# Attention and GRU kernel: a group's projections spread over its four steps, other work moved with them

## The reference

```python
x = x + attn(cond_layer(x, 1, rms_weight, cond, Wk, Wo, ln_gamma, ln_beta), W_attn, b_attn, W_proj, b_proj)
x = x + ffn(gru(cond, x, W_ih, W_hh, b_ih, b_hh), weight, scale_weight, bias)
```

## Time and profile before

| | us |
|---|---|
| median of three runs (lowest, highest) | 452.37 (450.24, 454.48) |
| profiled execution | 452.29 |
| its span, first to last instruction | 450.5 |
| TensorE busy (share of the span) | 408.1 (91%) |
| VectorE busy | 327.2 (73%) |
| ScalarE busy | 220.1 (49%) |
| GpSimd busy | 141.4 (31%) |

### The profile page before, as it was taken

The page is one execution under the profiler, slowest core; times in us unless marked ns, Lnnn a source line. Parts: engine busy times, 40 slices in busy tenths (PEclk is TensorE's granted clock), DMA queues, the critical chain, the costliest instruction groups (busy, mean ns, idle before and its releaser), DMA issues.

```text
span 450.5 us, 14909 instructions
## 1 busy us (share of the span) xinstructions
PE 408.1 (91%) x6216; PEld 339.5 (75%) x6216; DVE 327.2 (73%) x971; ACT 220.1 (49%) x545; POOL 141.4 (31%) x202
## 2 busy tenths in 40 slices
PE   8899898988969799889798779899999999999994
PEld 6556676766847677768567569799999999999984
DVE  2586989698876966868867955658676677667665
ACT  6265546555455465645565453444444444444341
POOL 6763174664364534624566730000000000000000
PEclk9999999999999989899999999999999999999999
DMA  8942413123132041231212000001010101000001
GB/s 289 397 167 95 130 45 113 50 73 84 38 98 93 28 119 50 73 102 43 74 52 73 26 3 0 1 2 47 2 47 1 47 8 43 23 25 25 24 25 70
DMA packets 33251, 30.46 MB, mean 68 GB/s; under 512 B 3104, under 2 KB 28320, under 8 KB 33184
## 3 DMA queue, kind: packets, MB, share of 16 engines
q1 hardware_dynamic: 33184, 29.51, 19.8%
HBM read 16.92 MB, written 8.39 MB: 56 GB/s over the span
## 4 chain that ended last, share of the span: by engine, by line
PE 72%; DVE 15%; issue 5%; ACT 5%; POOL 1%; DVEq 0%; POOLq 0%
PE ps_s L1428 7%; PE ps_t L1428 6%; PE ps_o L1428 6%; PE ps_s L1327 6%; PE ps_m L1365 5%; PE ps_t L1260 5%; PE ps_s L1483 5%; PE ps_t L1483 4%; PE ps_a L1483 4%; PE ps_a L1260 4%; PE ps_m L1483 4%; PE ps_o L1345 4%; DVE pT L964 4%; DVE mx L956 2%; PE ps_m L1357 2%
## 5 line engine op out<-in xcount | busy, mean ns | idle before, releaser
L533 POOL TENSOR_TENSOR sc<-masked,mx 128x512 f32<-128x512 f32 x64 | 66.4, 1059 | 102.4 <-DVE mx L956 102.4
L1365 PE MATMUL ps_m<-oT,w_p 128*128 128x128 f32 x256 | 38.0, 293 | 11.4 <-ACT oT L572 11.4
L1365 PEld LDWEIGHTS ps_m<-oT,w_p 128*128 128x128 f32 x256 | 31.8, 195 | 18.3 <-ACT oT L572 18.3
L948 DVE COPY_PREDICATED masked<-kst,ps_s 128x512 f32<-128x512 int32 x64 | 43.7, 731 | 1.5 <-PE ps_s L1327 1.5
L639 ACT ACTIVATE sc<-sc 128x512 f32<-128x512 f32 x64 | 39.9, 624 | 8.8 <-POOL sc L533 8.5
L964 DVE STREAM_TRANSPOSE pT<-sc 128x512 f32<-128x512 f32 x64 | 41.4, 682 | 1.4 <-ACT sc L639 1.4
L1327 PE MATMUL ps_s<-kbd,qn 32*32 32x128 f32 x2048 | 38.4, 272 | 2.6 <-issue 2.4
L956 DVE TENSOR_REDUCE mx<-masked 128x16 f32<-128x512 f32 x64 | 39.7, 660 | 0.0
L747 ACT ACTIVATE zg<-ps_t,brz 128x128 f32<-128x128 f32 x64 | 20.1, 365 | 39.6 <-PE ps_t L1428 37.3
L1094 DVE SCALAR_TENSOR_TENSOR rg<-ps_o,vec,rg 128x128 f32<-128x128 f32 x64 | 19.5, 345 | 24.8 <-PE ps_o L1428 23.9
L1428 PEld LDWEIGHTS ps_s<-hT,w_hh 128*128 128x128 f32 x256 | 33.1, 191 | 4.9 <-DVE hT L1112 2.8
(11 more groups left out here) (161 smaller groups left out, 811.4 us busy)
## 6 DMA issues: line engine op xcount, KB each, us to landing
xf<-in_x_feat SPq DMA_DIRECT2D x8, 512.0 KB, 9.5
xg<-in_x_tok SPq DMA_DIRECT2D x8, 512.0 KB
kbd<-kn SPq DMA_DIRECT2D x64, 64.0 KB, 1.9
v_dram<-vn SPq DMA_DIRECT2D x16, 256.0 KB, 2.6
vbd<-v_dram SPq DMA_DIRECT2D x64, 64.0 KB, 2.0
out_feat<-ost SPq DMA_DIRECT2D x16, 256.0 KB, 2.0
w_qkv<-in_wqkv SPq DMA_DIRECT2D x1, 768.0 KB, 9.8
w_ih<-in_wih SPq DMA_DIRECT2D x1, 768.0 KB, 13.3
```

Source lines behind the costliest of these rows:

```text
L533: nc.gpsimd.tensor_tensor(shifted, kept, m.unsqueeze(2).to_broadcast([P, NH // 2, S]), ALU.subtract).then_inc(sc_sub, 1)
L948: nc.vector.copy_predicated(kept, keep.unsqueeze(1).to_broadcast([P, NH // 2, S]), ps_s[:, h * 512:(h + 1) * 512].rearrange("p (h k) -> p ...
L1365: last = nc.tensor.matmul(ps_m[:, E + m * P:E + (m + 1) * P], w_p[:, c, m * P:(m + 1) * P], oT[:, c, :], start=(c == 0), stop=(c == C - 1))
```

## The change

On TensorE, `work_ahead` becomes `keys`, `queries` and `values`, and their halves are spread over the four steps: keys 0 at i = 0; keys 1 and queries 0 at i = 1; queries 1 and values 0 at i = 2; values 1 at i = 3. The second half of each stands ahead of the output projection of its step. The block projection of group g+2 moves from i = 1 to i = 0 for g = 1 to 5, ahead of the output projection, and into a bank of `ps_t` instead of `ps_a`; the VectorE and ScalarE operations around it move with it. On VectorE the token statistics are cut in two: tiles 0 and 1 stay at the end of step 2, tiles 2 and 3 with the aggregation go to step 3, where the transposition of the probabilities comes ahead of the mask. The adds giving y now follow the transposition of step 2. `inverse_std` moves to i = 3. On ScalarE the second exp of step 0 goes ahead of `oT`. SP's queue is as before.

```diff
         proj_ps = ps_a[0:MH, 0:E]
         proj_ps_1 = ps_s[0:MH, 0:E]
+        proj_ps_ahead = ps_t[0:MH, 0:E]
...
+                    if i == 3 and g + 2 < NG:
+                        inverse_std(g + 2)
                     if n + 1 < NT:
                         softmax_shift(n + 1)
-                    if i == 2 and g + 2 < NG:
-                        inverse_std(g + 2)
                     if n - 1 in BY_POOL:
                         residual(n - 1, (n - 1) // GT, (n - 1) % GT)
...
                 if i == 0 and not last_group:
                     round_y(g + 1, 0)
                     round_y(g + 1, 1)
+                    softmax_exp(n, n % 2, 1)
                 if n > 0:
                     attn_out(n - 1)
-                softmax_exp(n, n % 2, 1)
+                if i > 0 or last_group:
+                    softmax_exp(n, n % 2, 1)
+                if i == 0 and 0 < g < NG - 2:
+                    round_proj(g + 2, proj_ps_ahead)
+                if i == 1 and not last_group:
+                    k_chunk(g + 1, 1)
+                if i == 2 and not last_group:
+                    q_chunk(g + 1, 1)
+                if i == 3 and not last_group:
+                    v_half(g + 1, 1)
                 if n - 1 in BY_POOL:
                     projection_out(n - 1)
-                if i == 0 and not last_group:
-                    k_chunk(g + 1, 0)
                 if i == 0 and g in (0, 2):
                     cond_exp(2 + g // 2)
                 if i == 0 and not last_group:
-                    k_chunk(g + 1, 1)
+                    k_chunk(g + 1, 0)
                 if i == 1 and not last_group:
                     q_chunk(g + 1, 0)
-                    q_chunk(g + 1, 1)
-                if i == 1 and g + 2 < NG:
+                if i == 1 and g == 0:
                     round_proj(g + 2, proj_ps)
                 if i == 2 and not last_group:
                     v_half(g + 1, 0)
-                    v_half(g + 1, 1)
...
                 norm_ahead = g + 2 < NG
                 if n > 0:
                     normalise(n - 1)
+                if i == 0 and 0 < g < NG - 2:
+                    select_blocks(g + 2)
...
                 if i == 0 and g + 1 < NG:
                     rest_of_y(g + 1)
+                if norm_ahead and i == 3:
+                    some_token_stats(g + 2, 1).then_inc(bn_done, 1)
+                    mean_and_variance(g + 2)
+                    transpose_probs(n, n % 2)
                 if n + 1 < NT:
                     softmax_mask(n + 1, (n + 1) % 2)
-                if norm_ahead and i == 2:
-                    add_proj(g + 2, ps_a)
...
-                transpose_probs(n, n % 2)
+                if i == 0 and 0 < g < NG - 2:
+                    rest_of_proj(g + 2, proj_ps_ahead)
                 if i == 1 and g in (0, 2):
                     keep_weights(2 + g // 2)
-                if norm_ahead and i == 1:
-                    select_blocks(g + 2)
+                if not norm_ahead or i < 3:
+                    transpose_probs(n, n % 2)
+                if i == 1 and g == 0:
+                    select_blocks(2)
+                if norm_ahead and i == 2:
+                    add_proj(g + 2, ps_a)
                 if n + 1 < NT:
                     softmax_max(n + 1, (n + 1) % 2)
                 if norm_ahead and i == 2:
-                    token_stats(g + 2)
-                if norm_ahead and i == 2:
-                    mean_and_variance(g + 2)
+                    some_token_stats(g + 2, 0)
...
-                if norm_ahead and i == 1:
-                    rest_of_proj(g + 2, proj_ps)
+                if i == 1 and g == 0:
+                    rest_of_proj(2, proj_ps)
...
+            def queries(k, m):
+
+                if k > 1 and m == 0:
+                    pe.wait_ge(proj_lo, min(k + 2, NG))
+                if k > 0:
+                    pe.wait_ge(v_out, 2 * (k - 1) + m + 1)
+                project_qk(k, 0, q_mm, m)
+
+            def values(k, h):
+
+                if k > 0:
+                    pe.wait_ge(q_out, C * k + h + 1)
+                elif h == 1:
+                    pe.wait_ge(z_done, 3)
+                project_v(k, h)
...
                 if n > 0:
                     transpose_attn(n - 1)
+                if i == 0 and 0 < g < NG - 2:
+                    pe.wait_ge(v_out, 2 * g + 1)
+                    batch_proj(g + 2, proj_ps_ahead)
                 if norm_ahead and i == 2:
                     pe.wait_ge(k_out, 2 * g + 4)
                     spread_proj(g + 2, ps_a)
                 if i == 1 and g in (0, 2):
                     cond_col(2 + g // 2)
+                if i == 1 and not last_group:
+                    keys(g + 1, 1)
+                if i == 2 and not last_group:
+                    queries(g + 1, 1)
+                if i == 3 and not last_group:
+                    values(g + 1, 1)
                 if n > 0:
                     project_out(n - 1)
-                if i < 3 and not last_group:
-                    work_ahead(g + 1, i, 0)
-                    work_ahead(g + 1, i, 1)
+                if i == 0 and not last_group:
+                    keys(g + 1, 0)
+                if i == 1 and not last_group:
+                    queries(g + 1, 0)
+                if i == 1 and g == 0:
+                    pe.wait_ge(k_out, 2 * g + 3)
+                    batch_proj(2, proj_ps)
+                if i == 2 and not last_group:
+                    values(g + 1, 0)
                 if g + EARLY < NG and i == 3:
                     pe.wait_ge(z_done, 2 * g + 6)
                     block_products(g + EARLY)
-                if norm_ahead and i == 1:
-                    pe.wait_ge(k_out, 2 * g + 3)
-                    batch_proj(g + 2, proj_ps)
                 if i == 0 and g in (0, 2):
                     pe.wait_ge(c_sub, 3 + g // 2)
+                if i == 1 and g in (0, 2):
+                    pe.wait_ge(weights_kept, 1 + g // 2)
```

More of the change, by code:

```diff
@@ L900, in centre_half, with some_token_stats @@
                                                ALU.mult, ALU.mult).then_inc(centre_done, 1)
+            def some_token_stats(k, h):
+                dve.wait_ge(z_done, 2 * k + h + 1)
+                for i in range(h * TH, (h + 1) * TH):
+                    last = nc.vector.bn_stats(st[:, i, :], y[:, i, :])
+                return last
             def token_stats(k):
-                for i in range(GT):
-                    dve.wait_ge(z_done, 2 * k + i // 2 + 1)
-                    last = nc.vector.bn_stats(st[:, i, :], y[:, i, :])
-                last.then_inc(bn_done, 1)
+                some_token_stats(k, 0)
+                some_token_stats(k, 1).then_inc(bn_done, 1)
             def mean_and_variance(k):
@@ L1404, in _ @@
             pe.wait_ge(kw_out, 4)
[L1405 removed]
+            queries(0, 0)
             pe.wait_ge(b_out_done, 1)
             batch_proj(1, proj_ps_1)
[L1408 removed]
+            queries(0, 1)
             pe.wait_ge(k_out, C)
```

25 lines of the change are left out of this document (6 added, 19 removed).

## The result

| | before | changed kernel |
|---|---|---|
| median of four runs (lowest, highest), us | 453.19 (450.24, 454.48) | 441.33 (435.97, 443.33) |
| ratio to before, 95% interval | | 0.972 [0.966, 0.978] |
| profiled execution, its span, us | 452.29, 450.5 | 443.33, 441.5 |
| granted clock over the span | 0.992 | 0.987 |
| TensorE, VectorE busy, us | 408.1, 327.2 | 404.9, 330.7 |

The ratio leaves out the changed kernel's slowest execution, the profiled one (443.33 us, 1.7% above its fastest).

A forecast was written before the change was run, and what follows sets the result against it. TensorE was taken to bound steps 0 to 2 of a group, VectorE's chain step 3. Savings of 12.5, 6.0, 2.4 and 0.5 us, less 2 put back, made 19.4: 452.3 - 19.4 = 433 us, range 427 to 444.

The forecast's parts named there:

- A middle group: Groups 1 to 5: steps of 7.96, 5.97, 6.68 and 4.47 us, 25.1 in sum, against 28.1 undisturbed before.
- Group 6: Group 6 was to take 24.6 us against 27.03 before, saving 2.4 us.
- K's transfer: First half of kbd in at 8.3 us, wanted by the next group's scores at 12.65: slack 4.3 us, stays hidden.
- The rival with K late: Scores at the start of step 3 wait for K's first half, making the kernel slower: 458 us, chance 0.07.
- a chain through VectorE: VectorE's chain bounds every step: 0.6 us more a group, 436 us; with stalls 446 to 452, chance 0.11.
- `pT` held up in step 3: Probs product in step 3 waits for pT held up by exp: 1 us a group, 439 us; no separate chance.
- I put back 2 us: Unexplained stalls in step 3 of groups 3 and 4, 2.5 us, counted as gone; 2 us added back to the time.
- My upper bound of 5: Upper bound in us for the returning stalls: one in every other group and no cover.
- my own case: The forecast of 433 us with its own range of 427 to 439, chance 0.66.
- the clock rival: Idle time before the transposes of y in step 0 lowers the clock in every group: 7.5 us lost, 440, chance 0.16.
- The clock at 1.00 throughout: Expected sign: granted clock at 1.00; the forecast is wrong if it falls in more than one group.
- The smaller terms: Savings outside the middle: group 0 0.5 us, groups 1 and 2 3.0 each; group 7, prologue and GRU nothing.

The follow-up runs named there:

- the shift of 24: Changed kernel with one-column products replacing warm-up matmuls, so later TensorE instructions stand 24 weight loads further on: 444.25 us; placed in the prologue's idle time, 442.07 us.

## Why the prediction was right, and where it was off

- **A middle group.** 25.1 forecast, 25.3 measured (25.30 to 25.34 in twelve clean groups of five profiled executions). Steps 1 and 3 came to within 0.23, step 2 was 0.29 shorter than the pieces had it. Step 0 was 8.22 for 7.96: the scores began 2.70 us into it, as forecast, though only 0.88 of that was waiting; `pT` then released the probs product 7.50 us into the step, where I had 7.23. Only in group 2, with the cond chain, did step 0 pass the 9 us that the forecast had named as a sign of being wrong: 9.6, and 9.4 before. So the order of events was right, and part of the closeness is a sum in which step 2's error offset the others.
- **The parts.** Worked out, the change saves 28.0 - 25.3 = 2.7 us a clean group (3.0 forecast). From the runs: spreading 28.0 - 26.5 = 1.5, the statistics 1.1, the block projection 0.1. The last was to cover the `oT` wait in step 0; it does, and step 0 ends on `pT` anyway.
- **Group 6.** 24.6 forecast, 24.5 and 24.6 in the two kernels with the shift of 24 (one of them in the idle time), without a gap in it, 28.1 in the changed kernel.
- **K's transfer.** The slack of 4.3 us became 3.5 (169.4 to 172.9). No load of keys ended a wait of TensorE. The rival with K late fell. So did those of a chain through VectorE (TensorE did not wait for VectorE in steps 1 and 2 of the clean groups, and a clean group is 25.3 us for VectorE's 23.2 of work) and of `pT` held up in step 3, where no wait for it came in groups 1 to 6.
- **The step that failed** is "I count them as gone above; as I can't name their cause I put back 2 us". The stalls weren't a disturbance of step 3 that goes with the idle time there, to be counted as gone. They are late instruction fetches at places of the stream, moved by edits that add or take a matmul. In the profiled run they cost 4.7 us in group 5 (30.0 against 25.3) and 3.5 in group 6 (28.1 against 24.6), in group 5 with the low clock behind the gap. That is 8.2 us for the 2 put back. My upper bound of 5 was too low too. The measured 441.33 us so lies outside my own case, 427 to 439, and next to the 440 of the clock rival, whose mechanism hardly came. That the whole range held it owes something to luck: its upper part was there for other causes.
- **The clock at 1.00 throughout** failed as well, and by the forecast's own sign, since it fell in more than one group: 0.94 in group 0 behind the 1.93 us wait for `pT`, 0.94 in group 5 behind the 2.90 us gap, 0.93 in group 7. The first rival had named a lowered clock, with another cause: behind the waits for y, which it feared, the clock stood at 1.00 in groups 3 and 4.
- **The smaller terms.** Group 0 was to gain 0.5 and lost 0.9 (its first probs product ends at 51.9 instead of 51.1, behind the 1.93 us wait for `pT`, and the scores then ran slowly). Groups 1 and 2 saved 2.3 and 2.5 for 3.0 each. Group 7 takes 19.2 us for 18.4, the GRU 186.6 for 186.4, both booked at nothing.

The stall in group 3's last step before, 7.21 for 5.33 us, on which the forecast's 2 us rested, is itself such a gap. It stands at record 5313, on the grid, and ends 1.6 us after a fetch had landed, while `on` had been ready since 155.77:

```profile
156.84 0.41 PE L1357 MATMUL ps_m<-kst,on 128*128 128x128 f32 x2 [1.90 <-issue]
```

The ledger of the profiled run, above the forecast: group 5 4.9, group 6 3.5, group 0 1.4, groups 1 and 2 1.2, groups 3 and 4 0.4, group 7 0.9, GRU 0.2, less the 2 put back: 10.5 us. 433 + 10.5 is 443.5, and it took 443.33. The median of the four runs is 2 us below that one: their spans are 434.2, 438.7, 440.4 and 441.5 us at granted clocks of 0.996, 0.992, 0.986 and 0.987. The shortest of them is the one with the highest clock; its 435.97 us is 5 above the 431 of the forecast without stalls. It was not profiled, so its gaps are not known.

What stays open: why a fetch is late where no large load stands ahead of it, whether moving the `xg` load would clear the largest gap, and whether the stream could be laid out so that none falls anywhere. No kernel here was shown beyond doubt to beat the changed one; the one with the block projection back may.

## What to carry to other kernels

In an in-order queue the cost of an operation is what stands behind it. Four statistics, 1.4 us of VectorE, ahead of the small normalisation that all later work hung on, cost TensorE a wait of 1.21 us a group though VectorE had room; with half of them put behind it that wait was gone in group 3. And where the trace shows a gap in the midst of one uniform block, with nothing awaited, count all instructions of the engine up to it in two kernels and look when the instruction queue's fetch landed: if the counts agree and the times don't, it is the stream. Then a local gain is to be judged by the stretches that have no such gap, since the sum over the kernel changes by several us with any edit.

## What the runs showed of the hardware

- TensorE stands still for 0.5 to 3.4 us at some places of its instruction stream, multiples of 256 records apart, in every kernel profiled here (62 gaps, 3 to 13 us a kernel). One fetch of 16 KB for 258 records is counted in the same stretch, and each gap ends 1.22 to 1.59 us after a fetch has landed.
- The largest of them followed the traffic of a 512 KB load: the fetch began 3.2 to 4.2 us after the load's issue in the nine executions that have the gap, and ahead of its issue in four of the five that haven't. A shift of the stream by 24 loads cleared groups 3 to 6 (25.3, 25.3, 25.3, 24.5 us) and brought other gaps.
- A gap can cost more than its length. Behind the 2.90 us one the granted clock fell to 0.57 over 2.4 us, and the six keys products took 2.62 us instead of 1.66; the step lost 4.7 us.
- Products of a single column are no cheap filler. In the kernel shifted by 24 loads TensorE's timeline shows early in the prologue

```profile
7.73 3.77 PE L1403 MATMUL ps_s<-oT 128*128 128x1 f32 x17
```

so 0.2 us for each record there. All 32 of them took from 4.67 to 11.36 us, where the eight records of the 256-column warm-ups that they replaced had taken 2.6 us, and the prologue was 5.7 us longer.
